# 64-column w1 products, zeros and biases moved up, experts' inputs five pairs ahead, and settling in pairs of units with square roots on ACT

## What is computed

```
xn   = layernorm(x)
# layer 0, attention part (a batch is one chunk of 512 rows, so the scan's weight update is not needed)
q    = l2_normalize(heads(rms_norm(xn @ wq)));  o = w1 @ (silu(w0 @ q) * (w2 @ q))      # 4 heads of 64, 128 hidden
# layer 0, feed-forward part: top 2 of 16 experts, and 2 shared ones
s    = softmax(xn @ centroids.T + expert_biases);  g, e = top2(s)
ffn  = xn + sum_k g_k * (xn @ Wr[e_k].T + br[e_k]) + (xn @ Ws.T + bs) / 2
x1   = x + o + ffn
# layer 1
xn1  = layernorm(x1);  a = rms_norm(xn1) * (gamma + 1)
attn = softmax(q k.T / 8) v @ w_out            # 16 heads of 64, 512 x 512 per batch and head
out  = x1 + attn + (xn1 @ ternary(w_ffn).T) * alpha + bias
```

## Time and profile before

| | |
|---|---|
| three runs, us | 3041.45, 3036.73, 3049.71 |
| the profiled execution: time, span, us | 3047.77, 3046.0 |
| busy, share of the span | PE 91%, PEld 67%, DVE 69%, ACT 60%, POOL 66% |
| mean granted clock of PE | 0.952 |
| DMA | 282.95 MB, mean 93 GB/s |

### The profile page before, as it was taken

How to read it: one execution, slowest core, us unless ns; L and a number is a source line. 1 busy time by engine, 2 the same in 40 slices (tenths; PEclk the granted TensorE clock), 3 DMA queues, 4 the chain that set the end, 5 groups by cost and what they waited for, 6 DMA issues and landing times.

```text
span 3046.0 us, 46091 instructions
## 1 busy us (share of the span) xinstructions
PE 2774.1 (91%) x13314; PEld 2043.3 (67%) x13314; DVE 2111.6 (69%) x3578; ACT 1841.7 (60%) x2651; POOL 1995.8 (66%) x1246
## 2 busy tenths in 40 slices
PE   6999678555499999999999999999999999999997
PEld 4555377444366777777777777777777777777775
DVE  6878555688766666767676766667666666767663
ACT  4555222122267777767676777777777777777774
POOL 4666500477257777777777777777777777777775
PEclk9999899666699999999999999999999999999998
DMA  4432367798512232222222222232322222231321
GB/s 135 133 124 91 134 206 216 219 266 254 176 42 67 49 74 54 68 69 52 69 54 68 58 64 63 58 76 45 74 53 71 58 62 75 43 79 43 79 48 48
DMA packets 271646, 282.95 MB, mean 93 GB/s; under 512 B 97344, under 2 KB 214336, under 8 KB 271424
## 3 DMA queue, kind: packets, MB, share of 16 engines
q1 hardware_dynamic: 259264, 248.25, 30.8%
q0 software_dynamic: 12288, 33.57, 3.6%
HBM read 131.76 MB, written 82.31 MB: 70 GB/s over the span
## 4 chain that ended last, share of the span: by engine, by line
PE 70%; POOL 1%; DVE 1%; ACT 1%; DMA 0%; issue 0%; SPq 0%; POOLq 0%; ACTq 0%; DVEq 0%
PE psV_b L1581 8%; PE psV_b L1576 8%; PE psV_b L1577 8%; PE psS_b L1564 8%; PE psS_b L1563 7%; PE psN_b L1549 7%; PE psY_b L1504 4%; PE psX_b L1504 4%; PE psY_b L1505 4%; PE psY_b L1506 4%; PE psX_b L1505 4%; PE psX_b L1506 4%; POOL pp_lo_b L1294 1%; PE psN_b L1633 0%; DVE vals_lo_b L1472 0%
## 5 line engine op out<-in xcount | busy, mean ns | idle before, releaser
L1294 POOL TENSOR_TENSOR pp_lo_b<-pf_b,pp_hi_b 128x1024 fp32r<-128x1024 f32 x512 | 1229.7, 2402 | 604.3 <-ACT pp_hi_b L1336 517.9
L1440 DVE TENSOR_REDUCE negmax_b<-psN_b 128x2 fp32r<-128x1024 f32 x512 | 626.9, 1224 | 379.1 <-PE psN_b L1549 371.8
L1331 ACT ACTIVATE pf_b<-psS_b 128x1024 f32<-128x1024 f32 x512 | 526.1, 1028 | 238.4 <-PE psS_b L1564 235.2
L1563 PE MATMUL psS_b<-qA_b,kA_b 128*128 128x512 f32 x1024 | 405.8, 396 | 6.8 <-DVE qB_b L1455 5.0
L1564 PE MATMUL psS_b<-qB_b,kB_b 68*128 68x512 f32 x1024 | 406.6, 397 | 0.0
L1577 PE MATMUL psV_b<-pp_hi_b,vals_lo_b 128*64 128x512 f32 x1024 | 403.6, 394 | 0.0
L1576 PE MATMUL psV_b<-pp_hi_b,vals_hi_b 128*65 128x512 f32 x1024 | 402.0, 393 | 1.7 <-DVE vals_lo_b L1472 0.2
L1355 ACT ACTIVATE kA_b<-psX_b 64x512 fp32r<-64x512 f32 x256 | 152.0, 594 | 289.4 <-PE psX_b L1506 284.6
L1549 PE MATMUL psN_b<-kA_b,qA_b 128*128 128x512 f32 x1024 | 322.6, 396 | 4.7 <-DVE negmax_b L1440 4.2
L1581 PE MATMUL psV_b<-pp_lo_b,vals_hi_b 128*65 128x512 f32 x1024 | 320.2, 394 | 5.1 <-POOL pp_lo_b L1294 5.1
L1336 ACT ACTIVATE pp_hi_b<-pf_b 128x1024 fp32r<-128x1024 f32 x256 | 271.5, 1061 | 8.1
(11 more groups left out here) (209 smaller groups left out, 5623.6 us busy)
## 6 DMA issues: line engine op xcount, KB each, us to landing
kA_b<-kA_b SPq DMA_DIRECT2D x128, 256.0 KB, 3.2
qB_b<-qA_b SPq DMA_DIRECT2D x128, 256.0 KB, 2.9
inverse_b<-inverse_dram SPq DMA_DIRECT2D x256, 128.0 KB, 3.1
xs_e<-rows_dram SPq DMA_DIRECT2D x144, 128.0 KB, 2.6
results_dram<-ys_e SPq DMA_DIRECT2D x72, 256.0 KB, 2.4
x_a<-x_dram SPq DMA_DIRECT2D x16, 512.0 KB, 4.7
part_dram<-acc_a SPq DMA_DIRECT2D x32, 256.0 KB
acc_s<-part_dram SPq DMA_DIRECT2D x32, 256.0 KB
```

Of the source, the lines that this page charges most:

```text
L1294: pool.tensor_tensor(pp[1][:, c], pf[:, c], pp[0][:, c].bitcast(F32), ALU.subtract).then_inc(pl_pool, 1)
L1331: a.activation(pf[:, c], psS[:], ACT.Exp).then_inc(exp_act, 1)
L1440: v.tensor_reduce(negmax[:, n.slot(2), 2 * c:2 * c + 2], psN[:], AX.X, ALU.max, negate=True).then_inc(mx_dve, 1)
L1563: pe.matmul(psS[:, t], kA[:, s, keys], qA[:, s], start=True, stop=False)
```

## The change

Route. `w1` is [128, 4, 64], without zeros; the product of head j writes partitions 64j to 64j + 63 of psB, in one set of sums with the full products before it. Its memset goes, and one ACTIVATE in place of four fills it. SP at step 31 loads eight addresses at a time and writes all 16 zero tiles, and the table, ahead of the stores of sums; the biases' load moves from `experts` to step 17. Of DVE's sixteen `weights_low` four stand ahead of the first hidden product of step 31, four ahead of the second, eight at the end. Many tiles now share memory: raw weights lie in the biases' tile, and junk, z2, qn, qt and acc in the two rings of `Ahead`.

Experts. Loads run five pairs ahead (ring of 12), the wait for the biases goes, and in its last pairs SP loads the sums and x of the first three units of `settle` (`Ahead.load`).

Settle. Units go in pairs. Rings of six for sums, x, gathered rows and x1. PE adds x by an f32 product with the identity and transposes acc by f32 products (no transpose mode), all into psA (4 banks); the ternary product is one f32 product (`wtern` f32, `xrt` unsplit) in place of two fp32r ones. DVE loses L992, L975 and L1012. The square root of a pair is one ACT instruction with `Sqrt`; ten small DVE instructions a pair (one refines the root by a Newton step) take the place of six a unit. POOL has only gathers. One xT is stored in place of two halves. The stage waits for sums and base stores apart (`based`).

Phase_b. x comes unsplit into `raw_x` (two slots of ot's high half) at step 11, after the O units of the batch before; ACT makes the high half at the end of step 12 (`rows_high`), DVE the low one in two parts, at step 12 and step 13 (`rows_low`); for the first batch both stand behind the split of the first weight chunk. The bias of the feed-forward part, no longer in the base, is added by DVE at steps 3 to 6 of each batch, four instructions of 128 x 256. PE waits for `xl_dve` in place of the transfer.

```diff
-        self.wtern = sb("wtern", [P, KD, D], F32R)
+        self.wtern = sb("wtern", [P, KD, D])
...
+class Ahead:
+
+
+    RING = 6
...
+        self.acc = ctx.enter_context(nc.sbuf_tensor("acc_s", [P, self.RING, U, D], F32))
+        self.x = ctx.enter_context(nc.sbuf_tensor("x_s", [P, self.RING, U, D], F32))
...
+    def load(self, sp, u):
+        g, half = u // GU, u % GU * U * P
+        sp.dma_start(self.acc[:, u % self.RING], self.part[g * GU:(g + 1) * GU].rearrange("m p a b -> p m (a b)")[:, :, half:half + U * P]
+                     ).then_inc(self.a_in[u % self.RING], 16)
+        sp.dma_start(self.x[:, u % self.RING], self.x_dram[u]).then_inc(self.a_in[u % self.RING], 16)
...
-        w1 = sb("w1", [P, FH, P])
+        w1 = sb("w1", [P, FH, FD])
...
+                if v == 17:
+                    sp.wait_ge(tern_dve, 11)
+                    sp.dma_start(bias_bc[:], io["br"].rearrange("e n -> (e n)").partition_broadcast(P)).then_inc(br_in, 16)
+                if v == NU - 1:
+                    sp.wait_ge(tb_dve, 1)
+                    for h in range(2):
+                        at = nc.values_load_multi_w_load_instructions(
+                            ends_u[0:1, h * 8:(h + 1) * 8], engines=[mybir.EngineType.SP], min_val=0, max_val=NE * region - P,
+                            skip_runtime_bounds_check_because="an end is a region's base and a count of at most N rows", bass_reorder=False)[1]
+                        for e in range(8):
+                            sp.dma_start(rows[bass.ds(at[e], P), :], zeros[:]).then_inc(ends_in, 16)
+                    sp.wait_ge(tb_dve, 13)
...
-                    o = h % 2 * FD
-                    a.activation(w1[:, h, o:o + FD], raw_1[:, h], ACT.Copy, scale=0.5).then_inc(w1_act, 1)
+                a.activation(w1[:], raw_1[:], ACT.Copy, scale=0.5).then_inc(w1_act, 1)
 
...
+            def weights_low(first, end):
+                for c in range(first, end):
+                    at = weights_of_experts(c)
+                    v.wait_ge(wr_act, c + 1)
+                    v.tensor_tensor(raw[at].bitcast(F32R), raw[at], wr_hi[at].bitcast(F32), ALU.subtract).then_inc(wr_dve, 1)
...
+                    weights_low(0, 4)
...
+                    weights_low(4, 8)
...
+            weights_low(8, 16)
...
-                        pe.matmul(psB[:, 0], wshare[:, k, rows_m], tokens, start=(k == 0), stop=False)
...
-                        mm = pe.matmul(psB[:, 0], w1[:, 2 * m + j], th[:, first:first + 3:2, j], start=False, stop=(j == 1))
+                        mm = pe.matmul(psB[j * FD:(j + 1) * FD, 0], w1[:, 2 * m + j], th[:, first:first + 3:2, j], start=False, stop=True,
+                                       skip_group_check=True)
                     mm.then_inc(b_pe, 1)
...
-        XS = 8
+        XS = 12
...
+            for j in range(5 * U):
...
-            sp.dma_start(bias_bc[:], io["br"].rearrange("e n -> (e n)").partition_broadcast(P)).then_inc(br_in, 16)
...
                 for t in range(U):
-                    load((n + 3) * U + t)
+                    load((n + 5) * U + t)
                 need(sp, y_dve, U, n, U)
...
+                if n >= PAIRS - 5 and n < PAIRS - 2:
+                    ahead.load(sp, n - PAIRS + 5)
...
-                load(u + 3)
+                load(u + AR)
...
+                    sp.dma_start(xT_dram[b, :, :, at], xrt[:, u % 2, i]).then_inc(stored[u % 2], 16)
+                base_rows(u - 2)
...
                 if u == GU + 1:
                     for r in range(2):
-                        sp.wait_ge(stored[r], 80)
-                    sp.dma_start(early.xT[0][:].bitcast(F32), xT_hi[0]).then_inc(early.xt_in, 16)
-                    sp.dma_start(early.xT[1][:].bitcast(F32), xT_lo[0]).then_inc(early.xt_in, 16)
+                        sp.wait_ge(stored[r], 32)
+                    sp.dma_start(early.xT[1][:].bitcast(F32), xT_dram[0]).then_inc(early.xt_in, 16)
...
+                need(g, s_dve, SD, u - YR, 4)
+                for t in range(U):
+                    n = u * U + t
+                    for k in range(TOP):
+                        g.indirect_dma_start(out=y[:, u % YR, t, k], out_offset=None, in_=results[:, :],
+                                             in_offset=bass.IndirectOffsetOnAxis(ap=kept.place[:, k, n:n + 1], axis=0)
+                                             ).then_inc(y_in[u % YR], 16)
...
+            for u in range(NU):
                 gather(u)
...
+            for w in range(NW + 1):
+                for u in range(2 * w - 2, 2 * w):
+                    if u >= 0:
+                        need(a, f_dve, FC, w - 1, FC)
+                        need(a, t_pe, 1, u - 2, 1)
+                        for t in range(U):
+                            a.activation(xr[:, u % 2, t], x1[:, u % XR, t], ACT.Identity, bias=factor(u, SHIFT, t),
+                                         scale=factor(u, SCALE, t)).then_inc(x_act, 1)
+                for u in range(2 * w - 2, 2 * w):
+                    if u >= 0:
+                        need(a, t_pe, 1, u, 1)
+                        need(a, f_pe, 1, u - 2, 1)
+                        if u >= 2:
+                            a.wait_ge(stored[u % 2], 32 * (u // 2))
+                        a.activation(flat(xrt[:, u % 2]), psT[:, u % 2], ACT.Copy).then_inc(t_act, 1)
+                if w < NW:
+                    need(a, v_dve, 1, w, 1)
+                    need(a, f_dve, FC, w - 2, 3)
+                    a.activation(root[:, w % 2].rearrange("p a b -> p (a b)"), vs[:, w % 2].rearrange("p a b -> p (a b)"),
+                                 ACT.Sqrt).then_inc(s_act, 1)
...
+            def gathered(u):
+                if u >= NU:
...
-                v.tensor_tensor(acc[:, u % 4], psA[:, u % 2].rearrange("p (t d) -> p t d", t=U), x[:, u % 4],
-                                ALU.add).then_inc(s_dve, 1)
-                need(v, s_dve, SD, u, 1)
...
-                                           in1=acc[:, u % 4, t], op0=ALU.mult, op1=ALU.add).then_inc(s_dve, 1)
-                need(v, s_dve, SD, u, 3)
+                    v.scalar_tensor_tensor(out=acc[:, u % AR, t], in0=y[:, u % YR, t, 0], scalar=kept.share[0][:, n:n + 1],
+                                           in1=psA[:, u % 4, t * D:(t + 1) * D], op0=ALU.mult, op1=ALU.add).then_inc(s_dve, 1)
+                need(v, s_dve, SD, u, 2)
...
-                rows_low(u - 1)
-                v.tensor_tensor(x1b[:, u % 3], x1[:, u % 3], fbias_bc[:].unsqueeze(1).to_broadcast([P, U, D]),
-                                ALU.add).then_inc(s_dve, 1)
...
+
+            def variances(w):
+                need(v, s_dve, SD, 2 * w + 1, SD)
+                need(v, s_act, 1, w - 2, 1)
+                v.tensor_tensor(vs[:, w % 2], mv[:, w % 2, :, 1].unsqueeze(1).to_broadcast([P, 2, W]), eps[:], ALU.add).then_inc(v_dve, 1)
...
+            def factors(w):
+
+                f, (inverse, other, s) = fac[:, w % 2], [newton[:, i] for i in range(3)]
+                need(v, s_act, 1, w, 1)
+                v.reciprocal(inverse, root[:, w % 2]).then_inc(f_dve, 1)
+                need(v, f_dve, FC, w, 1)
+                v.scalar_tensor_tensor(out=other, in0=vs[:, w % 2], scalar=0.5, in1=inverse, op0=ALU.mult, op1=ALU.mult).then_inc(f_dve, 1)
+                need(v, f_dve, FC, w, 2)
+                v.scalar_tensor_tensor(out=s, in0=root[:, w % 2], scalar=0.5, in1=other, op0=ALU.mult, op1=ALU.add).then_inc(f_dve, 1)
+                need(v, f_dve, FC, w, 3)
+                v.reciprocal(f[:, 0], s[:, 0]).then_inc(f_dve, 1)
+                need(v, f_dve, FC, w, 4)
+                v.tensor_tensor(f[:, 1], f[:, 0], s[:, 1], ALU.mult).then_inc(f_dve, 1)
+                need(v, f_dve, FC, w, 5)
+                v.scalar_tensor_tensor(out=f[:, 2], in0=f[:, 1], scalar=LEAST, in1=s[:, 0], op0=ALU.max, op1=ALU.mult).then_inc(f_dve, 1)
+                need(v, f_dve, FC, w, 6)
+                v.reciprocal(f[:, SCALE], f[:, 2]).then_inc(f_dve, 1)
+                v.tensor_scalar(f[:, GAIN], f[:, 1], LEAST, kept.alpha_bc[:, 0:1], ALU.max, ALU.mult).then_inc(f_dve, 1)
+                need(v, f_dve, FC, w, 7)
+                v.scalar_tensor_tensor(out=f[:, SHIFT], in0=mv[:, w % 2, :, 0], scalar=-1.0, in1=f[:, SCALE],
+                                       op0=ALU.mult, op1=ALU.mult).then_inc(f_dve, 1)
+
+            for w in range(NW + 2):
+                gathered(2 * w)
+                if 0 <= w - 1 < NW:
+                    factors(w - 1)
+                finish(2 * w - 4)
+                gathered(2 * w + 1)
+                if w < NW:
+                    variances(w)
+                finish(2 * w - 3)
...
+                        pe.matmul(psA[:, u % 4, t * D:(t + 1) * D], kept.ident[:], x[:, u % AR, t], start=True, stop=False,
+                                  skip_group_check=True)
                         for m in range(KD):
                             at = (t * KD + m) * P
...
```

(50 more changed lines are left out.)

291 lines of the change are left out of this document (113 added, 178 removed).

## The result

The changed kernel takes 2933.72 us (2930.82 to 2943.91) beside 3043.66 us of the kernel before on the same chip: a ratio of 0.9645, 95% interval 0.9614 to 0.9677, 3.6% or about 108 us less. The prediction was 2952 us, range 2922 to 2990. The profiled execution has a span of 2931.8 us, 114.2 less than before.

A forecast was written before the change was run, and what follows sets the result against it. PE was taken to bound the attention loop and `route`, input waits to cost `experts` time, DVE to bound `settle` with DMA close behind; -18 -8 -4 -16 -46 +3 = -89 us from 3041.45 gives 2952 us, range 2922 to 2990.

The forecast's parts named there:

- 64 columns, -18: `route`: 64-column w1 products run two at a time, about 0.6 us saved a unit: -18 us, bounds -27 and 0.
- PE sets the pace: `route`: PE, busy 279 of 303 us with w1 loads 0.43 us apart, limits the stage; DVE is second.
- Zeros and L593, -8: End of `route`: earlier zero writes and weights_low let the last store go out at 356: -8 us, bounds -4 and -10.
- Biases, -4: `experts`: the biases' transfer behind `route`'s traffic removes the 4.87 us wait at the first `ys`: -4 us, bounds 0 and -5.
- Inputs five pairs ahead, -16: `experts`: 19.4 us of input waits go, less what reappears as DMA time: -16 us, bounds -5 and -22.
- Settling, -46: `settle`: DMA sets the pace at 5.6 us a unit, the stage ending at 761: -46 us, bounds -65 and -26.
- rival e: Best case: gathers bound `settle` at 5.0 us a unit and column halves save all 27 us; 2924 us, chance 0.08.
- The start of `phase_b`, +3: `phase_b`: x split +1.4 us, second table load +1.3 us, later batches 0; together +3 us, bounds 0 and +10.
- (a): `route`: column halves of the array do not overlap, so the -18 us goes; 2970 us, chance 0.18.
- (b): DMA bounds `experts` and `settle` harder: -16 becomes -5 and -46 becomes -26; 2983 us, chance 0.12.
- (c): `settle`: PE becomes the bound at half clock, 7.7 us a unit, no gain there; 2998 us, chance 0.04.
- (d): `settle`: PE at half clock and its order adds waiting, 9.7 us a unit, +77 us; slower, 3075 us, chance 0.03.

The follow-up runs named there:

- both orders: The changed kernel with two new orders in `route`, ACT's Exp one step later and PE's first counts psC behind the psR products: 2909.46 us, ratio 0.9551.
- the doubled stores: The changed kernel with every xT in `settle` stored twice, the second time to a tensor nobody reads: 2943.19 us, ratio 0.9667.

## Why the prediction was right, and where its steps were not

*64 columns, -18.* What was said of the array was right: PE's busy time fell by 15 us and the loads come four in a row. The step that failed is "PE sets the pace": I read it from 279 of 303 us busy and from loads right on each other within a psB group. The columns alone gave 4.5 us. The trace of before had the sign: two units took 19.6 us, of which PE was busy 18.5. The missing 1.1 us was for the most part PE waiting for DVE (rows from 45 to 338 us):

```profile
PE psC_a L621 <- DVE mask_a L480: 9.1, 14, 0.8
PE psG_a L609 <- DVE th_a L442: 7.8, 11, 2.3
```

I estimated DVE's floor as its busy time and gaps (8.7 us a unit) and left out that its waits for ACT and PE come round in a circle that shorter w1 products don't shorten.

*Zeros and L593, -8.* Right in kind and nearly in size: the zeros alone gave 10.

*Biases, -4.* The wait at the first `ys` went, and the stage is 8 us shorter by it, twice what was said; over the whole kernel the runs tell no difference.

*Inputs five pairs ahead, -16.* The cause was right, the size half of what it was: 32.7 us of stage. Three parts were mis-sized: the waits for inputs went altogether, and I gave back a part as "DMA time" by reckoning 1.7 us a pair at a full share, though `experts` now moves 272 GB/s and PE hardly waits; "issue", 9.0 us, was not counted at all; and PE's busy time for the same 1152 products fell by 11 us, of which a higher clock (0.95 to 0.96; 1.00 in after's middle) is some 3 and fewer interruptions are another 5 to 6, both estimates.

*Settling, -46.* 66 us, at the bound of -65 "at POOL's 5.0 a unit", which is the mechanism that came true (rival e for this stage). The failed step is DMA's 5.6 us a unit: 1.64 MB at 298 GB/s. It took the transfer rate of before, divided by its share, for a ceiling; after moved 304 GB/s from 530 to 660 us and the doubled stores 344. The terms of DVE (4.75 worked out, 4.87 seen when it sets the pace) and POOL (5.0 and 5.06) were right, and so was the clock: over 0.85 was asked, 0.91 came.

*The start of `phase_b`, +3.* 4.1 us came in all: 1.3 ahead of the first product, against the 1.4 worked out from L593 for the split of x, and 2.8 behind it, of which PE's longer wait for the Exp is 1.29, as taken from the row of the load. The other 1.5 are within what this stage differs by from trace to trace. The Trainium skill (ScalarE: Activation LUTs, What ACT_TABLE_LOAD costs) puts a switch at about 2.7 us, the load and a drain; the trace has the load of 1.28 us and the Exp right behind it (728.27 and 729.57), and PE's wait grew by no more than the load.

*Rivals.* (a) is refuted by the rows of L678. (b) and (c) did not come: experts and settle ran at 272 and 283 GB/s, and at clocks of 1.00 and 0.91. (d) neither. Of (e), the half on `settle` came true and the half on the columns didn't.

*The signs.* The w1 loads side by side, PE hardly waiting for inputs in `experts`, and the clock of `settle` came as said. `route` shorter by 26 us with the first load at 343 did not (12.6, and 356.8), nor did `settle` at 5.6 us a unit with DVE waiting for transfers (5.06, and 4.7 us of such waits in 160). So the number fell into the range with two of its mechanisms, PE's pace in `route` and DMA's in `settle`, not as they were told.

## What to carry to other kernels

An engine that is 92% busy need not set the pace: look at whether the remaining 8% recurs as one wait at one place, and follow that wait round; if it returns to an engine by way of instructions that are merely queued behind something that waits, change the order, which gave 1% here where the shorter products gave 0.14%. A share of DMA time is no measure of the room left. When one term of a stage is taken away, list the floor of every engine and believe the highest that is counted in instructions (POOL's gathers, here) sooner than one that is a rate; and look how far the second floor is, for here it stood at most 0.2 us a unit below the first.

## What the runs showed that was not expected

- The gathers' cost in DMA time was 3.8, 3.4 and 2.9 us per MB while all traffic went at 260, 304 and 344 GB/s (kernel before, after, and after with two stores).
- A pow of eight elements took 1.67 us on POOL in `settle`, with the roots back there, where one of four took 1.04 before.
- The wide w1 products on top of both orders made `settle`, two stages later and unchanged, 62 us slower in its trace (and all four runs slow by as much), with gaps of 1 to 20 us ahead of single instructions of PE, ACT and DVE. Its cause was not found.
